# The second feed-forward product of a two-layer decoder: float32 on one side, three bfloat16 pieces on the other

## The reference, cut to what matters

```python
def quantize_w8_per(w, axis):
    amax = jnp.clip(jnp.max(jnp.abs(w), axis=axis, keepdims=True), 1e-08, None)
    scale = 127.0 / amax
    w_q = jnp.clip(jnp.round(w * scale), -128.0, 127.0) / scale
def quantize_a16(x):
    amax = jnp.clip(jnp.max(jnp.abs(x)), 1e-08, None)
    scale = 32767.0 / amax
    x_q = jnp.clip(jnp.round(x * scale), -32768.0, 32767.0) / scale
W_in_sim = quantize_w8_per(W_in, axis=0)
W_out_sim = quantize_w8_per(W_out, axis=1)
x_sim = quantize_a16(x)
hidden = jax.nn.gelu(x_sim @ W_in_sim + b_in, approximate=False)
hidden_sim = quantize_a16(hidden)
out = hidden_sim @ W_out_sim + b_out
```

## Time and profile before

| | us |
|---|---|
| three runs: median (lowest to highest) | 3079.46 (3076.94 to 3079.56) |
| the profiled execution, its own time | 3080.45 |
| its span in the profile | 3078.5 |
| TensorE busy | 2708.3 (88%) |
| vector engine busy | 2054.1 (67%) |
| ScalarE busy | 1620.9 (53%) |
| GpSimd busy | 712.7 (23%) |

### The profile page before, as it was taken

How to read it: one execution, slowest core, us unless ns; L and a number is a source line. 1 busy time by engine, 2 the same in 40 slices (tenths; PEclk the granted TensorE clock), 3 DMA queues, 4 the chain that set the end, 5 groups by cost and what they waited for, 6 DMA issues and landing times. The chain is left out here.

```text
span 3078.5 us, 56653 instructions
## 1 busy us (share of the span) xinstructions
PE 2708.3 (88%) x20214; PEld 2029.4 (66%) x20231; DVE 2054.1 (67%) x3805; ACT 1620.9 (53%) x2699; POOL 712.7 (23%) x690
## 2 busy tenths in 40 slices
PE   8999889996896999999689999588988888476999
PEld 6777654453795888888577788455555555233888
DVE  5666648887343421111499999699999999676643
ACT  3333357876332222222366666499999999576000
POOL 0111104445474010101523320222222220200700
PEclk9999999998898999999899999699999999699999
DMA  4000162221775444444311110011111110145564
GB/s 131 1 1 1 46 213 80 84 84 55 281 261 196 145 140 146 140 144 150 106 35 42 38 38 8 24 27 29 29 29 29 29 29 15 49 202 209 186 187 150
DMA packets 159714, 291.61 MB, mean 95 GB/s; under 512 B 21008, under 2 KB 90640, under 8 KB 154896
## 3 DMA queue, kind: packets, MB, share of 16 engines
q1 hardware_dynamic: 133008, 228.99, 22.8%
q0 software_dynamic: 17792, 51.40, 5.1%
q10 hardware_dynamic: 8704, 8.39, 0.8%
HBM read 184.90 MB, written 103.81 MB: 94 GB/s over the span
## 5 line engine op out<-in xcount | busy, mean ns | idle before, releaser
L1293 ACT ACTIVATE cx_h<-bank,c_b 128x256 f32<-128x256 f32 (+1 forms) x288 | 117.3, 458 | 387.2 <-PE bank L1245 387.2
L1952 DVE TENSOR_SCALAR e_low<-bank 128x2048 f32<-128x2048 f32 x128 | 293.3, 2292 | 30.1 <-PE bank L1845 30.1
L1245 PE MATMUL bank<-cx_zT,cx_w 128*128 128x256 f32 (+1 forms) x1152 | 248.8, 369 | 1.9 <-DMA cx_w<-cw_dram 1.1
L1827 ACT ACTIVATE e_low<-e_low 128x2048 f32<-128x2048 f32 x128 | 244.7, 1912 | 4.1
L1256 PE MATMUL bank<-c_w,cx_h 128*128 x1088 | 246.6, 379 | 0.0
L1825 ACT ACTIVATE e_low<-e_low 128x2048 f32<-128x2048 f32 x128 | 243.6, 1903 | 0.0
L2325 PE MATMUL bank<-wout,fd_q 128*128 128x256 f32 x1024 | 224.3, 383 | 16.7 <-DVE fd_q L2344 16.7
L1245 PEld LDWEIGHTS bank<-cx_zT,cx_w 128*128 128x128 f32 x1152 | 211.1, 191 | 29.8 <-DMA cx_w<-cw_dram 1.5
L2325 PEld LDWEIGHTS bank<-wout,fd_q 128*128 128x128 f32 x1024 | 196.6, 192 | 44.5 <-DVE fd_q L2344 17.2
L1256 PEld LDWEIGHTS bank<-c_w,cx_h 128*128 128x128 f32 x1088 | 201.2, 190 | 24.4
L1845 PE MATMUL bank<-e_qT,e_kT 32*128 32x256 f32 x2048 | 148.9, 404 | 68.0 <-DVE e_high L1953 67.2
(11 more groups left out here) (371 smaller groups left out, 6242.3 us busy)
## 6 DMA issues: line engine op xcount, KB each, us to landing
cx_w<-cw_dram SPq DMA_DIRECT2D x72, 512.0 KB, 3.5
hidden<-fu_h SPq DMA_DIRECT2D x32, 1024.0 KB, 3.9
fd_h<-hidden SPq DMA_DIRECT2D x32, 1024.0 KB, 6.4
cx_rows<-expert_rows SPq DMA_DIRECT2D x64, 256.0 KB, 3.4
slot_y<-cx_y POOLq DMA_DIRECT2D x64, 256.0 KB, 2.6
g_cT<-ctxT_dram SPq DMA_DIRECT2D x32, 256.0 KB, 4.7
queries<-g_qT SPq DMA_DIRECT2D x32, 256.0 KB, 5.7
b_qT<-queries SPq DMA_DIRECT2D x32, 256.0 KB, 2.7
```

The costliest lines, as they stand in the source:

```text
L1245: last = nc.tensor.matmul(H[k][f // 2][:, (f % 2) * GROUP_ROWS:(f % 2) * GROUP_ROWS + cols], w1[k][:, c, f * P:(f + 1) * P], zT[k][:, c, 0 ...
L1827: nc.scalar.activation(flat(low[n % RING][:]), flat(low[n % RING][:]), ACT.Exp, scale=-1.0).then_inc(low_ready, 1)
L1952: nc.vector.tensor_scalar(flat(low[n % RING][:]), HEADS4.rearrange("p r s -> p (r s)"), -1.0, 0.0, ALU.mult, ALU.max).then_inc(neg_ready, 1)
```

## The change

The float32 product becomes three bfloat16 products, one for each piece of the other operand. The unit of work is a quarter of a trip: 2 of 8 chunks, for 512 rows (two batches); there are 64 units and rings of four buffers.

- ScalarE (`counted`) computes h * scale + MAGIC in float32, in place. The low 16 bits of each result are the whole number as int16; `counts` reads every second 16-bit value of the same tile.
- ScalarE (`weighed`) multiplies these counts by the row factor of W_out (`factor`, per partition) and rounds to bfloat16: the first piece.
- The vector engine (`remains`) computes counts * factor - first piece in float32; its upper 16 bits, read in place as bfloat16 (`upper`, every second value), are the second piece. `lowest` subtracts that, giving the third.
- TensorE multiplies each piece as the stationary operand with the whole numbers of W_out, now bfloat16, without the factor. Four row tiles a trip accumulate in four banks, alternating between two sets.
- The bias, times the scale, is split into three pieces likewise, laid in partitions 0, 32 and 64 of `pieces`, and one product with `pick` (ones in these rows) opens each bank. GpSimd keeps the maximum and sets `pick` and `pieces` up; it no longer touches X.
- The stores move to SP's queue, behind the loads; all loops are written out.
- In the experts stage the raw W_out gets a tile of its own (`s["wo"]`), and the last scaling goes.

The diff; removed lines of `ffn_down` are left out, since they stand in the listing above:

```diff
@@ -850,6 +850,7 @@
+I16 = mybir.dt.int16
@@ -872,7 +873,7 @@
-             "wi": sb("wi", [P, FC, D]),
+             "wi": sb("wi", [P, FC, D]), "wo": sb("wo", [P, FC, D]),
@@ -928,7 +929,7 @@
-            for dst, src in ((s["w2"], "cw2"), (s["b1"], "cb1"), (s["b2"], "cb2"), (s["wi"], "fwi"), (t["wout"], "fwo")):
+            for dst, src in ((s["w2"], "cw2"), (s["b1"], "cb1"), (s["b2"], "cb2"), (s["wi"], "fwi"), (s["wo"], "fwo")):
@@ -1316,8 +1317,8 @@
-            ch = Chain(dve, weight_steps, 14)
-            w = (s["wi"], t["wout"])
+            ch = Chain(dve, weight_steps, 13)
+            w = (s["wi"], s["wo"])
@@ -1371,8 +1372,6 @@
-                else:
-                    scaled(1, t["amax"])
@@ -2279,85 +2278,152 @@
     with ctx:
         sem = signals(nc, ctx, "fd_")
         sb = lambda n, shape, dt=FP: ctx.enter_context(nc.sbuf_tensor("fd_" + n, shape, dt))
...
+        QUARTERS, RING, WIDE = 4, 4, PAIR * S
+        CHUNKS, TILES, UNITS = FC // QUARTERS, PAIR * TB, TRIPS * QUARTERS
+        h = [sb(f"h{k}", [P, CHUNKS, WIDE]) for k in range(RING)]
+        high = [sb(f"high{k}", [P, CHUNKS, WIDE], BF) for k in range(RING)]
+        rest = [sb(f"rest{k}", [P, CHUNKS, WIDE]) for k in range(RING)]
+        low = [sb(f"low{k}", [P, CHUNKS, WIDE], BF) for k in range(RING)]
+        pick, pieces, bias, bias_rest = sb("pick", [P, P], BF), sb("pieces", [P, D], BF), sb("bias", [P, D]), sb("bias_rest", [P, D])
         topall = sb("topall", [P, 1])
...
+        (steps, all_ready, scale_ready, t_ready, high_ready, rest_ready, low_ready, o_raw, x_done, picked, bias_steps) = (
+            sem(n) for n in ("steps", "all", "scale", "t", "high", "rest", "low", "o_raw", "x_done", "picked", "bias"))
+        h_in = [sem(f"h_in{k}") for k in range(RING)]
         x_out = sem("x_out")
         rows_out = out.rearrange("(n p) d -> p n d", p=P)
...
+        sh, ish = s["scale"][:, 2:3], s["scale"][:, 3:4]
+        upper = lambda a: a.bitcast(BF)
+        counts = lambda k, f: h[k][:].bitcast(I16)[:, f, 0:2 * WIDE:2]
+        factor = lambda n, f: t["amax"][:, 1, n % QUARTERS * CHUNKS + f:n % QUARTERS * CHUNKS + f + 1]
+        O = lambda b: t["psum"][:, 2 * (b % 4):2 * (b % 4) + 2, 0:D]
+        BIAS_STEPS, PIECES = 6, (0, 32, 64)
         block = ctx.enter_context(nc.Block())
 
         @block.sync
         def _(sp):
...
+            def store(b):
+                tiles = slice(b * TB, (b + 1) * TB)
+                sp.wait_ge(x_done, b + 1)
+                sp.dma_start(rows_out[:, tiles, :], t["X"][:, tiles, :]).then_inc(x_out, 16)
+
+            for n in range(UNITS):
+                own = slice(n % QUARTERS * CHUNKS, (n % QUARTERS + 1) * CHUNKS)
+                if n >= RING:
+                    sp.wait_ge(high_ready, n - RING + 1)
+                    sp.wait_ge(rest_ready, n - RING + 1)
+                sp.dma_start(h[n % RING][:], hidden[n // QUARTERS][:, own, :]).then_inc(h_in[n % RING], 16)
+                if n % 2 and n >= 3 * QUARTERS:
+                    store(n // 2 - 6)
+            for b in range(B - 6, B):
+                store(b)
+            sp.wait_ge(x_out, 16 * B)
 
         @block.gpsimd
         def _(pool):
             nc.gpsimd.partition_all_reduce(topall[:], s["top"][:], P, ALL_MAX).then_inc(all_ready, 1)
...
+            nc.gpsimd.memset(pick[:], 0.0).then_inc(picked, 1)
+            nc.gpsimd.memset(pieces[:], 0.0).then_inc(picked, 1)
+            pool.wait_ge(picked, 2)
+            for row in PIECES:
+                nc.gpsimd.memset(pick[row:row + 1, :], 1.0).then_inc(picked, 1)
 
         @block.scalar
         def _(act):
...
+            act.wait_ge(scale_ready, 1)
+
+            def counted(n):
+                act.wait_ge(h_in[n % RING], 16 * (n // RING + 1))
+                nc.scalar.activation(h[n % RING][:], h[n % RING][:], ACT.Identity, scale=sh, bias=MAGIC).then_inc(t_ready, 1)
+
+            def weighed(n):
+                act.wait_ge(t_ready, n + 1)
+                if n >= RING:
+                    act.wait_ge(o_raw, n - RING + 1)
+                for f in range(CHUNKS):
+                    last = nc.scalar.activation(high[n % RING][:, f, :], counts(n % RING, f), ACT.Copy, scale=factor(n, f))
+                last.then_inc(high_ready, 1)
+
+            counted(0)
+            for n in range(UNITS):
+                if n + 1 < UNITS:
+                    counted(n + 1)
+                weighed(n)
 
         @block.tensor
         def _(pe):
...
+            def products(n, piece, pick_tile):
+                for m in range(TILES):
+                    for f in range(CHUNKS):
+                        last = nc.tensor.matmul(bank[TILES * (n // QUARTERS % 2) + m][:, 0:D], pick_tile(n, f, m), s["wout"][:, n % QUARTERS * CHUNKS + f, :],
+                                                start=False, stop=n % QUARTERS == QUARTERS - 1 and piece == 2 and f == CHUNKS - 1)
+                return last
+
+            first = lambda n, f, m: high[n % RING][:, f, m * P:(m + 1) * P]
+            second = lambda n, f, m: upper(rest[n % RING][:])[:, f, 2 * m * P + 1:2 * (m + 1) * P:2]
+            third = lambda n, f, m: low[n % RING][:, f, m * P:(m + 1) * P]
+
+            pe.wait_ge(picked, 2 + len(PIECES))
+            pe.wait_ge(bias_steps, BIAS_STEPS)
+            for n in range(UNITS):
+                if n % QUARTERS == 0:
+                    if n >= 2 * QUARTERS:
+                        pe.wait_ge(x_done, PAIR * (n // QUARTERS - 1))
+                    for m in range(TILES):
+                        nc.tensor.matmul(bank[TILES * (n // QUARTERS % 2) + m][:, 0:D], pick[:], pieces[:], start=True, stop=False)
+                pe.wait_ge(high_ready, n + 1)
+                products(n, 0, first)
+                pe.wait_ge(rest_ready, n + 1)
+                products(n, 1, second)
+                pe.wait_ge(low_ready, n + 1)
+                products(n, 2, third).then_inc(o_raw, 1)
 
         @block.vector
         def _(dve):
             dve.wait_ge(all_ready, 1)
             ch = Chain(dve, steps, 4)
...
             quantiser(nc, ch, topall, sh, ish)
             ch.end()
...
+            nc.vector.sem_inc(scale_ready, 1)
+            dve.wait_ge(picked, 2)
+            own = lambda a, row: a[row:row + 32, :]
+            odd = slice(1, 2 * D, 2)
+            bs = Chain(dve, bias_steps, BIAS_STEPS)
+            bs.did(nc.vector.tensor_scalar(bias[:], s["bo"][:], sh, None, ALU.mult)).see()
+            bs.did(nc.vector.tensor_copy(own(pieces, 0), upper(bias[:])[0:32, odd]))
+            bs.did(nc.vector.tensor_tensor(bias_rest[:], bias[:], upper(bias[:])[:, odd], ALU.subtract)).see()
+            bs.did(nc.vector.tensor_copy(own(pieces, 32), upper(bias_rest[:])[32:64, odd]))
+            bs.did(nc.vector.tensor_tensor(bias[:], bias_rest[:], upper(bias_rest[:])[:, odd], ALU.subtract)).see()
+            bs.did(nc.vector.tensor_copy(own(pieces, 64), own(bias, 64)))
+            bs.end()
+
+            def remains(n):
+                dve.wait_ge(high_ready, n + 1)
+                if n >= RING:
+                    dve.wait_ge(o_raw, n - RING + 1)
+                for f in range(CHUNKS):
+                    last = nc.vector.scalar_tensor_tensor(rest[n % RING][:, f, :], counts(n % RING, f), factor(n, f), high[n % RING][:, f, :], ALU.mult, ALU.subtract)
+                last.then_inc(rest_ready, 1)
+
+            def lowest(n):
+                dve.wait_ge(rest_ready, n + 1)
+                r = rest[n % RING]
+                nc.vector.tensor_tensor(low[n % RING][:], r[:], upper(r[:])[:, :, 1:2 * WIDE:2], ALU.subtract).then_inc(low_ready, 1)
+
+            def add(b):
+                x = t["X"][:, b * TB:(b + 1) * TB, :]
+                dve.wait_ge(o_raw, QUARTERS * (b // PAIR + 1))
+                nc.vector.scalar_tensor_tensor(x, O(b), ish, x, ALU.mult, ALU.add).then_inc(x_done, 1)
+
+            remains(0)
+            for n in range(UNITS):
+                if n + 1 < UNITS:
+                    remains(n + 1)
+                lowest(n)
+                if n % QUARTERS in (1, 2) and n >= QUARTERS:
+                    add(PAIR * (n // QUARTERS - 1) + n % QUARTERS - 1)
+            for p in range(PAIR):
+                add(B - PAIR + p)
+            dve.wait_ge(x_done, B)
 
 
 def build(nc, d, out):
@@ -2368,7 +2434,7 @@
-             "wi": sb("wi", [P, FC, D], BF), "wout": sb("wout", [P, FC, D]), "amax": sb("amax", [P, 2, FC]),
+             "wi": sb("wi", [P, FC, D], BF), "wout": sb("wout", [P, FC, D], BF), "amax": sb("amax", [P, 2, FC]),
```

More of the change, by code:

```diff
@@ L2316, in _ @@
         @block.tensor
         def _(pe):
-            nc.tensor.sem_inc(o_raw, PAIR)
-            with pe.Fori(0, TRIPS) as i:
-                for p in LANES:
-                    pe.wait_ge(q_ready, batch_of(i, p))
-                    pe.wait_ge(x_done, batch_of(i, p))
-                    for n in range(TB):
-                        for f in range(FC):
```

(30 more changed lines are left out.)

10 lines of the change are left out of this document (removed).

## The result

| | before | after |
|---|---|---|
| three runs: median (lowest to highest), us | 3079.46 (3076.94 to 3079.56) | 3037.13 (3033.90 to 3038.62) |
| profiled execution: own time / span, us | 3080.45 / 3078.5 | 3033.90 / 3031.8 |
| ratio of the runs, 95% interval | | 0.9864 (0.9844 to 0.9883) |
| last stage: from the maximum over partitions to the end of the span, us | 239.0 | 195.4 |

The kernel is 1.4% faster: 42.3 us by the medians. In the two profiles the last stage is 43.6 us shorter. It also began 3.1 us earlier (2836.42 against 2839.49), but one profile cannot tell so little: in this kernel and four variants that differ from it only behind that point the stage began at 2836.4, 2839.7, 2839.7, 2841.0 and 2839.3.

The account below looks back on a forecast made before the run. TensorE's float32 product was taken as the bound. After 2851.6, 172.2 us of products, 1.5 for clock and 2 for coupling end TensorE at 3027.3; additions and tail give span 3031.8, forecast 3033 us, range 3022 to 3062.

Parts of the forecast that it names:

- The bound before: Last stage, second feed-forward product: TensorE's float32 product bounds it, 224.28 us without a break.
- the saving on TensorE: Last stage: bfloat16 products 0.109 us apart, 2.73 us a unit, 174 us of TensorE work in place of 224.
- rival 3: TensorE in the last stage: weight loads not hidden, all 1600 in series add 157 us, giving 3190; chance 0.04.
- The rule that the prediction weighed: TensorE: weight loads overlap products only when going to other row groups, leaving full-array loads bare; the change would lose.
- The vector engine: Last stage: remains, lowest and half an addition take 2.66 us a unit, 0.07 below TensorE, nearly a tie.
- 16-bit view, integer input: Last stage: reading every second 16-bit value and integer input priced as existing rows; ends half and double.
- Rival 2: Vector engine, last stage: reading every second 16-bit value costs more; at double price 142 us more, 3175; chance 0.11.
- mild half of rival 2: Vector engine, last stage: such reading at 1.15 times the price, unit 3.0 us, time 3050; chance 0.04.
- DMA: Last stage's hidden-value loads: landing in 3.5 to 4.2 us, keeping pace while within 4.4; the plan's thinnest margin.
- the 2 us that I had set aside for all coupling: Last stage: loss for the near tie with the vector engine and first units without stock; ends 0 and 10.
- Nothing for GpSimd's bias addition: Removing GpSimd's bias addition, 54.7 us, gains nothing, since it ran beside TensorE.
- The 1.5 us for the clock: Start of the last stage's product: TensorE at half clock costs 1.5 us; ends 0 and 4.

Follow-up runs that it names:

- e9: Changed kernel with the vector engine's first operation (remains) multiplying by constant 1.0 instead of the column of row factors; last product at 186.9 us of the stage.
- e6: Changed kernel with remains reading float32 values side by side instead of every second 16-bit value; 747 ns an operation, last product at 189.6 us.
- e1: Changed kernel with eight buffers for the loaded hidden values in place of four; last product at 187.8 us of the stage, ratio to before 0.9851.
- e7: Changed kernel with GpSimd adding the bias to X again and TensorE's bias products removed; last product at 219.6 us of the stage.
- e4: Changed kernel with the first piece written in float32 and read in place, remains one operation of 1024 elements; last product at 184.7 us, ratio to before 0.9849.
- e5: Changed kernel with the stores moved back from SP's queue to ScalarE's; last product at 188.8 us of the stage.
- e11: The changed kernel itself, measured again; last product at 190.5 us of the stage, ratio to before 0.9852.
- e2: Changed kernel with the third piece computed for only one of two chunks and used twice by TensorE; last product at 186.7 us of the stage.
- e3: Changed kernel with 192 third-piece products left out on TensorE; last product at 191.1 us of the stage.

## Why the prediction was right, and where not

- **The bound before, and the saving on TensorE**: as written. 0.109 us a product was measured: a trip of 100 takes 10.91 to 10.92. The weight loads are hidden, also for the piece read every second value (99 ns); rival 3 is dead. The rule that the prediction weighed (the Trainium skill, TensorE: Matmul & The Clock Gate, Part 3, "Packing small matmuls") does not hold here: products with 1536 full-array loads of 98 to 99 ns between them started 0.109 us apart.
- **The vector engine** was mis-sized. I took 0.60 us from start to start for remains, by the row of an operation with a constant scalar (692 ns), while the row with a column scalar, the addition's 744 ns, stood beside it and was used for the addition alone. It measured 0.66 (742 ns; e9: 684 without the column). So a unit is 2.79 us and not 2.66, and the order of the two engines is reversed: it, not TensorE's 2.73, sets the pace once the stock is gone. By e9 that term is worth 3.9 us (190.8 against 186.9), at the late clock of both.
- **16-bit view, integer input**: free on the vector engine (e6); ScalarE's 707 and 1148 ns came out near the 0.7 and 1.15 foretold. Rival 2 did not happen: the view costs nothing. The vector engine did become longer by the column scalar, but to 2.79 us a unit, where the mild half of rival 2 had 3.0.
- **DMA**: a landing of 3.5 to 4.2 us was foretold against a limit of 4.4; the median was 4.1, up to 6.1. The loop did touch the limit: 3.0 us, by e1, more than the 2 us that I had set aside for all coupling, inside its ends of 0 and 10. It is no addition to the 3.9 of the vector engine: with the column scalar gone (e9) late loads cost nothing.
- **Nothing for GpSimd's bias addition.** Right for the kernel before, where TensorE covered it. But I did not ask what it would cost if left beside the new vector work: 29 us, by e7. Two thirds of the 43.6 us stand on this part of the change, at the price of 7 us of bias products on TensorE.
- **The sum.** The last product was foretold at 187.8 of the stage (3027.3 less 2839.5) and came at 190.8. Without the 2 us for coupling the sum gives 185.8, and e9, where TensorE sets the pace, measured 186.9: the start, the clock and the products are 1.1 us over, the first product being on time (7.3 us into the stage, as foretold). The vector engine with the loads cost 3.9 where 2 were set aside. That is the 3 us. The 1.5 us for the clock, with ends of 0 and 4, fit: the first trips of two executions of this kernel, with the late and the early clock, differ by 1.7 us. The span, 3031.8, was met to the digit by luck, as the stage began 3.1 us early in that execution. The median, 3037.13, is 4 us above the forecast of 3033, within the range.

## What to carry to other kernels

When a bound is removed, price the next engine by rows with the same kind of operands, a column scalar included: here 60 ns an operation reversed which of two nearly tied engines was the bound. Before leaving an idle engine's helpful work beside a newly full vector engine, look whether both read SBUF; work that cost nothing under the old bound can eat two thirds of the gain. And take stage times from the stage's own start: the stages ahead moved by 4.6 us between profiles, as much as most of the effects studied here. Look at the granted clock of both profiles before a gain of 2 us in a stage is put down to an edit.

## What the runs showed of the hardware that I had not expected

- A GpSimd addition beside two-source vector operations adds about 1 us to each, one for one: 747 to 1749 ns, and 1220 to 2281 ns.
- A column scalar costs the vector engine 62 ns an operation (684 against 746 ns); taking every second 16-bit value costs it nothing (747 against 747), nor does it slow TensorE's weight loads (98 to 99 ns).
- The granted clock rose to its upper level 10 us into the stage in three profiles (e4, e5, e11) and 16 us into it in seven (after, e1, e2, e3, e6, e7, e9); the changed kernel itself is in both groups. Where the vector engine set the end this made 0.3 us (190.8, 190.5); where TensorE did, about 2 (e2 and e9 at 186.7 and 186.9, e4 at 184.7).
